# Gathered and returned rows by indirect DMA, and weight chunks laid out as 128 runs of 8 KB, in a graph network with a mixture of experts

## The reference, cut to what matters

```
p = softmax(u @ gate_w + gate_b)            # 8 experts
keep the two largest p of each token
for each expert e: the 93 tokens (capacity) with the largest p[:, e] go to it, ties by index
    y = gelu(u_e @ w1[e] + b1[e]) @ w2[e] + b2[e]      # 512 -> 2048 -> 512
    x[those tokens] += p[those tokens, e] * y
```

## Time and profile before

| | us |
|---|---|
| median of 3 runs | 2194.7 (2192.68 to 2194.94) |
| the profiled execution | 2190.48 |
| its span, first to last instruction | 2188.6 |
| PE busy in it | 2114.8 (97%) |
| DVE busy | 1507.9 (69%) |
| ACT busy | 1123.9 (51%) |
| POOL busy | 855.9 (39%) |

### The profile page before, as it was taken

How to read it: one execution, slowest core, us unless ns; L and a number is a source line. 1 busy time by engine, 2 the same in 40 slices (tenths; PEclk the granted TensorE clock), 3 DMA queues, 4 the chain that set the end, 5 groups by cost and what they waited for, 6 DMA issues and landing times.

```text
span 2188.6 us, 36234 instructions
## 1 busy us (share of the span) xinstructions
PE 2114.8 (97%) x13402; PEld 1968.5 (90%) x13402; DVE 1507.9 (69%) x3184; ACT 1123.9 (51%) x3011; POOL 855.9 (39%) x687
## 2 busy tenths in 40 slices
PE   8887799999899999999999999999999999999998
PEld 7766566669779999999999999999999999999997
DVE  8737689854456767677776767777676676767676
ACT  4534556632455554455555445555554555555454
POOL 0000000000145555455555544555554455555461
PEclk9888899999999999999999999999999999999999
DMA  6000688871021231111122111112221111231110
GB/s 212 1 20 5 222 280 277 279 261 32 9 82 62 86 99 63 62 62 62 63 85 99 64 62 62 62 62 83 101 64 62 63 62 62 81 102 65 59 44 24
DMA packets 85688, 197.44 MB, mean 90 GB/s; under 512 B 5937, under 2 KB 10321, under 8 KB 85511
## 3 DMA queue, kind: packets, MB, share of 16 engines
q1 hardware_dynamic: 85512, 195.12, 26.5%
HBM read 193.75 MB, written 1.35 MB: 89 GB/s over the span
## 4 chain that ended last, share of the span: by engine, by line
PE 89%; ACT 4%; DVE 4%; DMA 1%; issue 1%; POOL 1%; SPq 0%; DVEq 0%; POOLq 0%; ACTq 0%
PE PS L54 80%; PE PS L53 5%; PE PS L57 3%; ACT HW L88 1%; ACT GT L88 1%; DMA WB<-w_rows 1%; DMA X<-in_x 0%; ACT HS L88 0%; DVE SM L107 0%; POOL SM L60 0%; DVE OHs L68 0%; DVE JU L66 0%; DVE M L75 0%; DVE OHd L69 0%; DVE SM L75 0%
## 5 line engine op out<-in xcount | busy, mean ns | idle before, releaser
L54 PE MATMUL PS<-ZH,WS 128*128 128x314 f32 x4096 | 946.4, 311 | 0.0
L54 PEld LDWEIGHTS PS<-ZH,WS 128*128 128x128 f32 x4096 | 692.2, 189 | 0.0
L54 PE MATMUL PS<-ZL,WS 128*128 128x314 f32 x2048 | 626.1, 306 | 0.0
L60 DVE TENSOR_TENSOR ACC<-ACC,PS 128x314 f32<-128x314 f32 x1008 | 476.4, 477 | 196.7 <-PE PS L54 186.8
L54 PEld LDWEIGHTS PS<-ZL,WS 128*128 128x128 f32 x2048 | 387.7, 189 | 0.0
L60 POOL TENSOR_TENSOR WS<-RAW,WS 128x512 fp32r<-128x512 f32 x256 | 326.5, 1296 | 116.6 <-ACT WS L88 116.6
L60 POOL TENSOR_TENSOR ZS<-ZS,ZQ 128x628 f32<-128x628 f32 x128 | 198.4, 1550 | 230.7 <-ACT ZQ L88 230.4
L60 POOL TENSOR_TENSOR ML<-MF,MH 128x400 fp32r<-128x400 f32 x124 | 130.9, 1056 | 363.6 <-ACT MH L88 363.6
L88 ACT ACTIVATE ZH<-PS,g1T 128x628 fp32r<-128x628 f32 x128 | 100.5, 785 | 313.5 <-PE PS L54 313.5
L88 ACT ACTIVATE EE<-EE,SM 125x100 f32<-125x100 f32 x640 | 233.0, 376 | 0.1
L88 ACT ACTIVATE MF<-PS 128x400 f32<-128x400 f32 x128 | 64.7, 506 | 315.8 <-PE PS L53 315.8
(11 more groups left out here) (338 smaller groups left out, 3731.3 us busy)
## 6 DMA issues: line engine op xcount, KB each, us to landing
RAW<-in_L_ffn_wz_w SPq DMA_DIRECT2D x66, 1024.0 KB, 6.0
RAW<-in_L_ffn_w SPq DMA_DIRECT2D x64, 1024.0 KB, 7.6
RAW<-in_L_ffn_Wq_w SPq DMA_DIRECT2D x32, 1024.0 KB, 8.5
CB<-c_rows SPq DMA_DIRECT2D x32, 195.3 KB
RAW<-in_L_gnn_W SPq DMA_DIRECT2D x4, 1024.0 KB, 8.9
RAW<-in_L_ffn_Wkv_w SPq DMA_DIRECT2D x4, 1024.0 KB, 5.4
RAW<-in_L_ffn_Wk_T SPq DMA_DIRECT2D x2, 1024.0 KB, 5.3
WB<-w_rows SPq DMA_DIRECT2D x6, 305.2 KB
```

The costliest lines, as they stand in the source:

```text
L54: return self.q.matmul(o, l, r, start=start, stop=stop)
L60: return Nothing() if self.q is None else self.q.tensor_tensor(out=o, in0=a, in1=b, op=op)
```

## The change

**Rows in.** The normalised rows `MU` are written to DRAM once (`x_rows`, ten DMAs). The small product of `PO` with `WSP` gets two more columns, which hold the token's number, and so gives for each place the number of its token (`IX`). POOL fetches the rows of an expert with one indirect DMA of 94 rows of 2 KB into `XR`, one of two buffers. Only expert 0 still gets its rows as products. The small product moves one expert ahead: `dispatch(e + 1)` stands after the first chunk of expert `e`. The transposes of `PO` are gone but for expert 7.

**Rows out.** The scaled output `OS` is plain fp32. SP writes it to DRAM (`y_rows`, two DMAs per expert, 0 to 6). Ten small operations on DVE (`places`, in expert 5) work out for each token the rows in `y_rows` of its lower and its higher expert among 0 to 6, row 0 (zeros) where there is none. POOL fetches them with five indirect DMAs each into `YL` and `YH`, and DVE adds them into `X` during expert 7. Expert 7 still goes the old way.

**Ranks.** `WB` has two buffers, and the row of expert `e` waits for the sum of expert `e - 2`. The row of expert 2 is issued before the loop.

**Weights.** The host lays out each 1 MB chunk so that each of the 128 partitions reads one run of 8 KB. Before, a partition read four runs of 2 KB, and two of 4 KB for `L1_ffn_wz_w1`.

```diff
+    def gather(self, dst, src, index):
+        if self.q is None:
+            return Nothing()
+        return self.q.indirect_dma_start(out=dst, out_offset=None, in_=src, in_offset=bass.IndirectOffsetOnAxis(ap=index, axis=0))
...
+        srcs = [I["L0_gnn_W1"][0], I["L0_gnn_W2"][0]]
...
+            k = slot_of(n)
+            return q.dma(RAW[k][:, :, :].rearrange("p a b -> p (a b)"), srcs[n]).then_inc(s_raw[k], 16)
...
+        xrow = nc.dram_tensor("x_rows", (625, D), f32, kind="Internal").ap()
+        yrow = nc.dram_tensor("y_rows", (1 + 7 * CS, D), f32, kind="Internal").ap()
...
             def load_row(e):
-                q.wait_ge(*rank_v.of(e - 1, "sum"))
-                q.dma(WB[:, :], wrow[e:e + 1, :].broadcast_to([P, 625])).then_inc(s_wrow, 16)
+                q.wait_ge(*rank_v.of(e - 2, "sum"))
+                q.dma(WB[e % 2][:, :], wrow[e:e + 1, :].broadcast_to([P, 625])).then_inc(s_wb[e % 2], 16)
+            def outputs(e):
+                q.wait_ge(*os_hi.of(e))
+                for lo, hi in ((0, 80), (80, CS)):
+                    q.dma(yrow[1 + CS * e + lo:1 + CS * e + hi, :], OS[lo:hi, e % 2, :]).then_inc(s_yw[e % 2], 16)
+            q.wait_ge(*mconst.of("zero"))
+            q.dma(yrow[0:1, :], ZR[:, :]).then_inc(s_rows, 16)
...
+                for lo, hi in ((0, 120), (120, 125)):
+                    q.dma(xrow[P * t + lo:P * t + hi, :], MU[lo:hi, t, :]).then_inc(s_rows, 16)
...
+            load_row(2)
             for m in range(64):
                 q.wait_ge(*w_used.of(m))
                 load(q, N_MOE + 8 + m)
                 if m == 2:
-                    load_row(2)
+                    load_row(3)
+                if m % 8 == 6 and m // 8 + 4 < NE:
+                    load_row(m // 8 + 4)
+                if m % 8 == 7 and m // 8 < NE - 1:
+                    outputs(m // 8)
...
+            q.wait_ge(s_rows, 16 * (2 * T5 + 1))
+            for e in range(1, NE):
+                k = e % 2
+                q.wait_ge(*sw_v.of(e, "index"))
+                if e >= 2:
+                    q.wait_ge(*xg_t.of(e - 2))
+                q.gather(XR[:, k, :], xrow, IX[k][:, :]).then_inc(s_xr[k], 16)
+            q.wait_ge(*code_v.of("low"))
+            q.wait_ge(s_yw[0], 32 * 3)
+            q.wait_ge(s_yw[1], 32 * 3)
+            for t in range(T5):
+                q.gather(YL[:, t, :], yrow[0:1 + 6 * CS, :], IL[:, t:t + 1]).then_inc(s_back, 16)
+            q.wait_ge(*code_v.of("high"))
+            q.wait_ge(s_yw[0], 32 * 4)
+            q.wait_ge(s_back, 16 * T5)
+            for t in range(T5):
+                q.gather(YH[:, t, :], yrow, IH[:, t:t + 1]).then_inc(s_back, 16)
...
+                if 2 <= e < NE - 1:
+                    q.wait_ge(s_yw[k], 32 * (e // 2))
+                q.act(OS[:, k, :] if e < NE - 1 else OSH[:, :], OT[:, :], ACT.Copy, scale=sw[k][:, 3:4]).then_inc(*os_hi.up(e))
...
+                q.cp(IX[k][:, :], PS[0:CS, 3, 2:3]).then_inc(*sw_v.up(e, "index"))
+                q.cp(sw[k][:, 0:2], PS[0:CS, 3, 0:2]).then_inc(*sw_v.up(e, "two"))
                 q.wait_ge(*sw_v.of(e, "two"))
-                q.tt(sw[k][:, 2:3], sw[k][:, 0:1], sw[k][:, 1:2], ALU.add).then_inc(*sw_v.up(e, "sum"))
+                q.tt(sw[k][:, 3:4], sw[k][:, 0:1], sw[k][:, 1:2], ALU.add).then_inc(*sw_v.up(e, "sum"))
...
+            def places():
+                def step(i, name):
+                    return i.then_inc(*code_v.up(name))
...
+                step(q.ts(CD[0][:, :, :], ranks, float(CAP), None, ALU.is_lt), "fits")
+                step(q.stt(CD[1][:, :, :], ranks, 1.0, EO[:, :, :], ALU.add, ALU.add), "row")
+                after_("fits")
+                step(q.stt(CD[0][:, :, :], chosen, 0.0, CD[0][:, :, :], ALU.is_ge, ALU.mult), "kept")
...
+                step(q.stt(IL[:, :], LH[0][:, :], 1000.0, LH[2][:, :], ALU.add, ALU.mult), "low")
...
+                if e:
+                    q.wait_ge(*os_hi.of(e - 1))
                 q.tt(OT[:, :], PS[0:CS, 2, :], B2[:, k, :], ALU.add).then_inc(*ot_v.up(e))
-                q.wait_ge(*os_hi.of(e))
-                q.stt(OSL[:, k, :], OT[:, :], sw[k][:, 2:3], OS[:, k, :].bitcast(f32), ALU.mult, ALU.subtract).then_inc(*os_lo.up(e))
...
+            def back(Y, n, name):
+                q.wait_ge(s_back, 16 * n)
...
+                    if name == "high":
+                        q.wait_ge(*x2_done.of("low", t))
+                    q.tt(X[:, t, :], X[:, t, :], Y[:, t, :], ALU.add).then_inc(*x2_done.up(name, t))
...
             for e in range(NE):
                 n = 6 * e
-                if e:
-                    combine(e - 1)
                 weights(n + 4)
+                if 1 <= e < NE - 1:
+                    dispatch(e + 1)
                 gelu(e, 0)
                 weights(n + 5)
+                if e == NE - 3:
+                    places()
                 if e + 2 < NE:
                     rank_tiles(e + 2, (0, 1))
                 gelu(e, 1)
+                if e == 0:
+                    dispatch(1)
                 weights(n + 6)
                 if e + 2 < NE:
                     rank_tiles(e + 2, (2, 3))
...
                 if e + 2 < NE:
                     rank_tiles(e + 2, (4,))
                     rank_end(e + 2)
-                if e + 1 < NE:
-                    dispatch(e + 1)
+                if e == NE - 1:
+                    back(YL, T5, "low")
                 weights(n + 8)
                 if e + 1 < NE:
                     gathered_T(e + 1)
                 weights(n + 9)
                 if e == NE - 1:
                     v_counts(q)
+                    back(YH, 2 * T5, "high")
...
             def dispatch(e):
-                k = e % 2
                 q.wait_ge(*rank_v.of(e, "po"))
-                q.wait_ge(*free[4])
-                q.wait_ge(*free[5])
-                for t in range(T5):
-                    o = PS[0:CS, 4, P * t:P * t + P] if t < 4 else PS[0:CS, 5, 0:P]
-                    i = q.tr(o, PO2[:, k, t, :].bitcast(f32), ident[0:P, 0:P])
-                i.then_inc(*pt_t.up(e))
-                free[4] = free[5] = pt_done.of(e)
-                q.wait_ge(*free[7])
+                q.wait_ge(*free[3])
                 q.wait_ge(*gate_v.of("wsl"))
                 for t in range(T5):
-                    i = q.mm(PS[0:CS, 7, 0:2], PO2[:, k, t, :], WSP[:, t, e, :], t == 0, t == 4)
+                    i = q.mm(PS[0:CS, 3, 0:4], PO2[:, e % 2, t, :], WSP[:, t, e, :], t == 0, t == 4)
                 i.then_inc(*sw_mm.up(e))
-                free[7] = sw_v.of(e, "two")
-                q.wait_ge(*free[6])
-                for i, xf in enumerate((XFH, XFL)):
-                    for t in range(T5):
-                        q.wait_ge(*(xfl_done.of(t) if i else xfh_done.of(t)))
-                        j = q.mm(PS[0:CS, 6, :], PO2[:, k, t, :], xf[:, t, :], t == 0 and i == 0, t == 4 and i == 1)
-                j.then_inc(*ga_mm.up(e))
-                free[6] = ga_done.of(e)
+                free[3] = sw_v.of(e, "two")
+            def slots_T():
+                q.wait_ge(*free[3])
+                q.wait_ge(*free[4])
+                for t in range(T5):
+                    o = PS[0:CS, 3, P * t:P * t + P] if t < 4 else PS[0:CS, 4, 0:P]
+                    i = q.tr(o, PO2[:, (NE - 1) % 2, t, :].bitcast(f32), ident[0:P, 0:P])
+                i.then_inc(*slots_mm.up("turned"))
+                free[3] = free[4] = slots_a.of("turned")
             def gathered_T(e):
-                q.wait_ge(*ga_done.of(e))
+                if e:
+                    q.wait_ge(s_xr[e % 2], 16 * ((e + 1) // 2))
...
             for e in range(NE):
                 up(e, 0)
-                if e:
-                    combine(e - 1)
+                if 1 <= e < NE - 1:
+                    dispatch(e + 1)
                 up(e, 1)
                 gelu(e, 0)
                 up(e, 2)
+                if e == 0:
+                    dispatch(1)
                 gelu(e, 1)
                 up(e, 3)
                 gelu(e, 2)
+                if e == NE - 1:
+                    slots_T()
                 down(e, 0)
                 gelu(e, 3)
-                if e + 1 < NE:
-                    dispatch(e + 1)
                 down(e, 1)
                 down(e, 2)
                 if e + 1 < NE:
                     gathered_T(e + 1)
                 down(e, 3)
             pe_keys(q, (0, 1))
-            combine(NE - 1)
+            combine()
             pe_keys(q, (2, 3))
...
+_ROW_CHUNKS = dict(L0_gnn_W1=4, L0_gnn_W2=4, L0_ffn_w2=4, L1_gnn_W1=4, L1_gnn_W2=4, L1_ffn_Wq_w=4, L1_ffn_wz_w1=2,
+                   L1_ffn_wz_w2=4, L1_ffn_Wk_T=4)
+_COLUMN_CHUNKS = ("L0_ffn_w1", "L1_ffn_Wkv_w")
...
+    def chunks(name, a):
+        if name in _ROW_CHUNKS:
+            k = _ROW_CHUNKS[name]
+            return a.reshape(-1, k, 128, 2048 // k).transpose(0, 2, 1, 3).reshape(-1, 128, 2048)
+        if name in _COLUMN_CHUNKS:
```

(49 more changed lines are left out.)

160 lines of the change are left out of this document (79 added, 81 removed).

## The result

The changed kernel takes 2197.4 us (median of 20 runs, 2192.8 to 2202.8), the kernel before, run beside it, 2193.8 (20 runs). The ratio is 1.0016, 95 % interval 1.0009 to 1.0022: no faster, and if anything slower, by 3.6 us. The forecast was 2146 us. The profiled execution has a span of 2195.3 us; before it was 2188.6.

A forecast was written before the change was run, and what follows sets the result against it. PE sets the pace, DVE and transfers having little to spare. Savings 16.0 + 21.7 + 3.2 + 6.3 + 1.7 = 48.9 us turn the profiled 2190.5 into 2141.6; with 4.2 for the median, 2146 us, own range 2139 to 2153 (wide 2138 to 2171).

The forecast's parts named there:

- The gather ... both ends cost nothing.: Expert loop: index ready at 8 us, PE asks for XR at 22.4, so the gather's 14.3 us are free; cost 0.
- 0 to 4.8, I take 0: Gather for expert 1: only about 9 us free, so a cost of 0 to 4.8 us, taken as 0.
- The rival of the late gather: XR gather takes 17 us instead of 14.3, 24 us lost, 2170; chance 0.14 together with the late return.
- the late return: Results for YH in expert 7: five POOL gathers at 5 us each lose 9 us, 2155; 0.14 with late gather.
- the late chunks: Rival that transfers bind the expert loop: at 323 GB/s the period is 28.8 us, 12 us lost, 2158; chance 0.13.
- I take the transfers as hidden.: Expert loop: 9.3 MB per 26.5 us, 350 GB/s, fits under the 377 and 422 seen with a full queue; cost 0.
- The layout: ... I take 0.: Weight chunks in 8 KB runs: 0, from 1 us better at the start to 1 worse; a later gather named, unpriced.
- YH: "Nothing.": Expert 7's sums of returned rows: OSL ready at 480.6, PE asks at 481.02, so no cost.
- The first expert: Expert 0: rank row wait gone, DVE runs from its split at 221.0, expert 2 of the order starts at 242.3; saves 16.0 us.
- PE's lost work: Per expert PE sheds dispatch 4.39 and combine 2.39, keeps 0.5: from 31.93 to 25.65 us.
- the loop of 26.5 us set by DVE: Expert loop: DVE needs 3.4 + 2.2 + 20.95 = 26.5 us against PE's 25.65; 5.4 saved each for experts 1 to 4.
- The row's wait of 11.6 us: PE's wait in the first expert, traced to expert 2's late rank row, goes; rival that it stays: 2157, chance 0.05.

The follow-up runs named there:

- experiment 8: Changed kernel with bias row and row gathers in 96 partitions, rank row and result gathers in 128: 2147.8 us, ratio 0.9794.
- experiment 4: Changed kernel with the bias row written to 96 and the rank row to 128 partitions instead of 94 and 125: 2185.4 us, ratio 0.9959.
- experiment 1: Changed kernel with the weight layout of before (runs of 2 and 4 KB): 2191.7 us, ratio 0.9995 to the kernel before.
- experiment 6: Changed kernel with the old layout, and bias and rank rows written to 96 and 128 partitions: 2169.0 us, ratio 0.9897.
- experiment 2: Kernel before with only the new layout of weight chunks, runs of 8 KB: 2192.9 us, ratio 0.9996.
- experiment 11: Changed kernel with bias and rank rows and all gathers in 96 and 128 partitions, and the old layout: 2146.1 us, ratio 0.9781.
- experiment 12: Changed kernel with rows and all gathers in 96 and 128 partitions, expert 1's index one step earlier on DVE: 2150.5 us, ratio 0.9808.
- experiment 10: Changed kernel with bias and rank rows in 96 and 128 partitions, row gathers in 96, result gathers still in 125: 2167.2 us, ratio 0.9892.
- experiment 14: Changed kernel with bias and rank rows in 96 and 128 partitions, row gathers in 96, result gathers in 127: 2210.3 us, ratio 1.0068.
- experiment 3: Changed kernel with experts 1 to 7 reading only the last quarter of each weight chunk: 2165.1 us, ratio 0.9875.
- experiment 5: Kernel before with only the rank rows in two buffers and row 2 asked for ahead of the loop: 2180.0 us, ratio 0.9947.

## Why the prediction was wrong

- **"The gather ... both ends cost nothing."** This step failed. 14.3 us were free, and the bound from above, 13.75 us, was that of a repeated row in another queue. The gather landed in 17.6 us (median), its 94 rows on 2 of 16 engines, beside long runs in the other queue, and PE waited 22.5 us for gathered rows. For expert 1, "0 to 4.8, I take 0" was 12.58. The rival of the late gather had 17 us for it and 24 us of waits (2170), with no word on the number of engines. Each rival was priced alone; the late gather, the late return and the late chunks came together.
- **"I take the transfers as hidden."** Half failed. The average rate was reachable: 341 GB/s at full speed of the loop in experiment 8, 398 from 410 to 440 us there, so the limit of about 358 GB/s in the Trainium skill (DMA: Bandwidth & Descriptors, Specifications) is not this kernel's. But the reasoning took a transfer as bytes over 16 engines, and ACT waited 44.7 us for chunks. By their counts of partitions the bias row lies on 2 engines and the rank row on 5 (packets show the rule for the gathers; for these two it is what experiment 4 gained). The earlier trace rows already showed 305 KB taking 13.75 us, and I read it as waiting behind chunks; written to 128 partitions it landed in 8.2 us (experiment 4). An estimate: at 26.5 GB/s an engine moves 0.70 MB in 26.5 us. Its share of the chunks is 0.52, and an engine that carries a part of the bias row (0.10), the rank row (0.06) and the gathered rows (0.10) has 0.78 to move. Which engines carry them was not looked at. It cost 12.1 us beside the other fault, 25.5 once that was mended.
- **"The layout: ... I take 0."** Failed, and in the direction that the prediction had named itself and given no price: beside narrow gathers the runs of 8 KB cost 5.7 us (experiment 1), and 16.4 with the rows wide (experiments 4 and 6). Only in the kernel before and with all four widths mended was it 0 (experiments 2 and 11).
- **YH: "Nothing."** Failed, 15.8 us. The rival "return is late" gave 9 us by POOL's issue time, which was small (five gathers in 7.8 us); the landing, 17.2 us each on 5 engines, was what took long, and YH's had to wait for YL's.
- **The first expert.** The split of weights forecast at 221.0 came at 225.10, since DVE waited 3.82 us for PE ahead of the rank row of expert 1 where it had waited 1.62. PE's timeline of experiment 12 shows the place, and the row of its stretch has the granted clock (0.50) as the third number from the end:

```profile
208.84 0.96 PE L54 MATMUL PS<-WSP,PO 125*94 125x4 f32 x5 [2.98 <-DVE PO L68]
209.66 2.43 PE L54 MATMUL PS<-XFH,PO 125*94 125x512 f32 x5
211.88 2.34 PE L54 MATMUL PS<-XFL,PO 125*94 125x512 f32 x5
```

```profile
209.00:214.00 5.00, 5.00 (x15) 3.59 (x16) 2.84 (x11) 0.00 (x0) 0.00 (x0) 0.50 0.19 59
```

In before the same two rows of five products had 1.38 and 1.32 us, at a granted clock of 1.00 from 206 to 212 us. 0.50 is the lower clock level, and it comes and goes from one execution to the next: in the profiles of experiments 6, 8, 10, 11 and 14, with the same instructions here, the row with XFH took 1.36 to 1.38 us. In experiment 8 the split came at 225.46 all the same; there the clock had stayed at 0.50 from 196 to 208 us. Of all kernels with the change only that of experiment 6 had it in time, at 220.95. What decides when the clock rises was not tested. So even with all widths mended expert 1 started at 247.1 (experiment 12) and not at 242.3.
- **What held.** PE's lost work, and the loop of 26.5 us set by DVE: the gathers of experiments 3 and 8 are issued 26.6 us apart, and PE waited 5.4 us in 5 places for XGL in 8. The row's wait of 11.6 us held too (13.8 us in experiment 5). With the four widths mended the kernel takes 2147.8 us, 1.8 from the forecast, but that this is so near is in part luck. The combine, forecast at 432.1, came at 442.04 there and at 439.06 in experiment 12, whose profiled execution took 2150.45 us against the 2141.6 that the sum had given for one. So the sum of compute was right to 7 to 10 us of the 49, and what it assumed of the DMAs was not.

## What to carry to other kernels

Before a DMA is priced by its bytes, count its partitions: if its slowest dimension has no divisor near 16, its time is that of a few engines, and other transfers are late with it. Pad to a multiple of 16 (94 to 96, 125 to 128) even though it moves more. Do not judge a second edit (here the layout) before that is done: it gave 0, 5.7 or 16.4 us, by the widths beside it. Where two transfers are narrow, mend both before judging either, and do not read a high DMA share as a full bus: look at GB/s at that share. A landing time taken as a bound must be that of the same shape and queue.

## What the runs showed of the hardware

- A gather into 127 partitions runs at 25 to 27 GB/s when it is alone and two of them at 53; with ten of them this kernel takes 62.6 us more than with 128.
- With its queue full of runs of 8 KB the core read 424 GB/s (26 to 38 us), and of 2 KB 389 (the same stretch of before), but the kernel of experiment 8, which moves 341 in its loop, runs the same with either (experiment 11).
- A gather of 94 rows landed in 17.6 us beside runs of 8 KB and in 10.7 beside runs of 2 and 4 KB; of 96 rows in 7.9 and 7.7. With the bias and rank rows wide, the 94 rows took 16.5 and 14.0. The length of the other queue's runs was felt by the narrow gather alone.
- POOL was busy 1.48 us with a gather of 94 rows, 0.92 with one of 96 (the first of a kernel took 3.07 and 2.64) and 2.55 to 5.12 with one of 127.
- While PE stood idle from 466 to 474 us in the 127 kernel its granted clock was 0.50, the level of 1.2 GHz; after a wait of 12.58 us in the changed kernel it worked at 0.50 from 253.87 to 259.00.
